# Attention stage of a four-block kernel: GpSimd adds the coarse weights to the fine ones in place, and one set of wide products sums them

## The reference

```python
for lvl, (ql, kl, vl) in enumerate(qkvs):
    if lvl == 0:
        A = jnp.exp(S)                                  # S masked, less its row maximum
        y = jnp.einsum('bnij,bnjd->bnid', A, vl)
        Av = A.sum(-1)
    else:
        A = jnp.exp(S)                                  # q of odd blocks, k of even blocks
        y = jnp.einsum('bnij,bnjd->bnid', A, v1b)
        Av = A.sum(-1)
        y, Av = each padded with zeros to even blocks, and repeated 2 ** lvl times
    seq_key = (idx >> lvl << lvl) + (2 ** lvl - 1)
    keep = seq_key <= idx                               # the last token of each group of 2 ** lvl
    Ysum = Ysum + jnp.where(keep[None, :, None], y, 0.0)
    Asum = Asum + jnp.where(keep[None, :], Av, 0.0)
out = Ysum / (Asum + EPS)[..., None]
```

## Time and profile before

| What | us |
|---|---|
| median of 3 executions | 697.13 |
| lowest and highest | 693.63 and 697.72 |
| the profiled execution, its own time | 694.56 |
| its span in the trace | 692.7 |

### The profile page before, as it was taken

One profiled execution on the slowest core, in us unless ns is written; L12 is line 12 of the kernel. 1 busy time (PEld: TensorE's weight loads), 2 busy tenths in 40 slices (PEclk: granted clock), 3 DMA queues, 4 the chain that ended last, 5 costly groups with the idle time before them and its releaser, 6 DMA issues.

```text
span 692.7 us, 17766 instructions
## 1 busy us (share of the span) xinstructions
PE 531.0 (77%) x6946; PEld 317.5 (46%) x6948; DVE 435.2 (63%) x881; ACT 286.8 (41%) x621; POOL 247.8 (36%) x247
## 2 busy tenths in 40 slices
PE   0768686474758997289999999999997656569991
PEld 0213232143434433157777677777766544344330
DVE  1477969883513564647788888878788466125552
ACT  3442432234114664465444455444444152127660
POOL 1367767652270666310111111211111223704662
PEclk9998797855698999599999999999999556979997
DMA  5999200000061883300001000001000000525854
GB/s 146 395 382 106 30 1 0 0 1 0 11 188 35 216 238 106 100 12 14 18 18 34 17 18 18 18 18 30 21 7 8 1 0 1 157 76 147 229 174 136
DMA packets 43601, 54.16 MB, mean 78 GB/s; under 512 B 10816, under 2 KB 34176, under 8 KB 42496
## 3 DMA queue, kind: packets, MB, share of 16 engines
q1 hardware_dynamic: 40960, 47.78, 24.9%
q0 software_dynamic: 2560, 5.26, 2.1%
HBM read 43.55 MB, written 9.48 MB: 77 GB/s over the span
## 4 chain that ended last, share of the span: by engine, by line
PE 65%; DVE 12%; issue 7%; ACT 5%; POOL 5%; DMA 2%; another core or an unknown queue 2%; SPq 1%; DVEq 0%; POOLq 0%; ACTq 0%
PE psum L1291 9%; PE psum L900 7%; PE psum L1309 6%; PE psum L1372 5%; PE psum L1346 4%; PE psum L1330 4%; PE psum L916 4%; PE psum L857 3%; PE psum L865 3%; DVE arena L621 3%; PE psum L907 2%; POOL arena L529 2%; PE psum L1362 2%; PE psum L257 2%; PE psum L1354 2%
## 5 line engine op out<-in xcount | busy, mean ns | idle before, releaser
L1640 POOL TENSOR_TENSOR arena<-arena 128x1024 f32<-128x1024 f32 x16 | 37.8, 2362 | 211.0 <-DVE arena L1562 211.0
L1135 POOL DMA_INDIRECT y_tok<-arena,to x48 | 55.2, 1149 | 70.8 <-ACT arena L976 65.8
L1291 PE MATMUL psum<-arena 128*128 128x512 f32 x128 | 62.8, 633 | 1.3 <-ACT arena L1429 1.0
L529 POOL TENSOR_TENSOR arena<-arena 128x512 f32<-128x512 f32 x32 | 51.4, 1628 | 30.3 <-DVE arena L621 30.3
L1446 ACT ACTIVATE arena<-psum 128x512 f32<-128x512 f32 x64 | 38.1, 597 | 37.2 <-PE psum L1291 37.2
L621 DVE TENSOR_TENSOR_SCAN arena<-arena 128x512 f32<-128x512 f32 x32 | 53.0, 1698 | 0.0
L900 PE MATMUL psum<-experts,arena 128*32 x96 | 50.0, 602 | 2.9 <-issue 1.9
L900 PE MATMUL psum<-arena 128*32 128x512 f32 x288 | 50.9, 605 | 0.0
L1309 PE MATMUL psum<-arena 128*128 128x128 f32 x384 | 46.6, 278 | 1.0 <-ACT arena L1451 1.0
L1570 DVE TENSOR_TENSOR x_tok<-x_tok,psum 128x512 f32<-128x512 f32 x32 | 22.0, 688 | 39.5 <-PE psum L1372 39.5
L981 ACT ACTIVATE arena<-experts 128x768 f32 x48 | 40.4, 845 | 14.3 <-issue 14.2
(11 more groups left out here) (197 smaller groups left out, 1185.2 us busy)
## 6 DMA issues: line engine op xcount, KB each, us to landing
arena<-in_experts SPq DMA_DIRECT2D x48, 384.0 KB
experts<-in_experts SPq DMA_DIRECT2D x8, 1536.0 KB, 19.5
arena<-sorted_x SPq DMA_DIRECT2D x48, 64.5 KB
sorted_x<-zeros SPq DMA_DIRECT2D x2, 1536.0 KB, 22.5
arena<-in_w_qkv SPq DMA_DIRECT2D x16, 192.0 KB, 3.2
arena<-y_tok SPq DMA_DIRECT2D x8, 256.0 KB, 3.7
arena<-in_w_out SPq DMA_DIRECT2D x16, 64.0 KB, 1.9
out<-x_tok SPq DMA_DIRECT2D x4, 256.0 KB, 2.7
```

The lines of the kernel that those rows point to most:

```text
L529: pool.tensor_tensor(a_g[m % HALF], a_r[c % 2], a_state[:, m, 0:CHUNK], ALU.mult).then_inc(s["g"], 1)
L1135: pool.indirect_dma_start(out=y_tok, out_offset=bass.IndirectOffsetOnAxis(ap=f_to[:, s:s + 1], axis=0), in_=f_gy[s % 4], in_offset=None).t ...
L1291: pe.matmul(ring("in", n, j)[:, :], b_w[n % 2][:, which * P:which * P + P], x, start=True, stop=True)\
```

## The change

The 22 narrow Z products of each unit are gone. GpSimd adds the coarse weights onto the fine ones inside b_e (merge), in five additions for each unit: 256, 128, 64, 32 and 32 elements in each partition, the last in half of the partitions. Each addition reads 16 neighbouring coarse weights at a time and 16 fine ones that stand 2, 4, 8, 16 or 32 columns apart, and writes these in place. From the second on, each waits for the one before. The four wide Z products then sum fine and coarse weights together (add_weights), and stand behind the Y products of weighted(n, ROUGH).

The additions of unit n wait for its coarse exponentials (expd) and for its fine Y products, which read b_e before it is changed (weighed, a new semaphore that counts twice in each unit behind the Y products). summed now counts once in each unit. copy_y and the drains of the values wait for weighed in place of summed. On GpSimd, merge(n+1) stands behind the product of unit n.

```diff
+        MERGES = LEVELS
...
+        def merged_columns(a):
+            fine = a[:, 0:2 * CHUNK].rearrange("p (h t) -> p h t", h=2)
+            rough = a[:, 2 * CHUNK:QK].rearrange("p (h i k) -> p h i k", h=2, k=D_B)
+            one = rough[:, :, 0:2].rearrange("p h i (g s) -> p h (i g) s", s=16)
+            two = rough[:, :, 2].rearrange("p h (g s) -> p h g s", s=16)
+            three = rough[:, :, 3, 0:32].rearrange("p h (g s) -> p h g s", s=16)
+            return [(fine.rearrange("p h (g c s) -> p h g c s", c=32, s=2)[:, :, :, 16:32, 1], one),
+                    (fine.rearrange("p h (g c s) -> p h g c s", c=32, s=4)[:, :, :, 16:32, 3], two),
+                    (fine.rearrange("p h (g c s) -> p h g c s", c=32, s=8)[:, :, :, 16:32, 7], three),
+                    (fine[:, :, 256 + 15:512:16], rough[:, :, 3, 32:48]),
+                    (fine[64:128, :, 31:512:32], rough[64:128, :, 3, 48:64])]
...
-                if not rough:
-                    after(pe, h["z_out"], n)
-                    for head in range(2):
-                        for r in range(2):
-                            rows, out = slice(64 * r, 64 * r + 64), slice(64 * head, 64 * head + 64)
-                            mm = pe.matmul(Z[r][out], b_ones[rows], b_e[n % 2][rows, head * CHUNK:head * CHUNK + CHUNK],
-                                           start=True, stop=False)
-                else:
-                    for i in range(part.start, part.stop):
-                        for head in range(2):
-                            for r in range(2):
-                                rows, out = slice(64 * r, 64 * r + 64), slice(64 * head, 64 * head + 64)
-                                for cols, place in places(r, i):
-                                    mm = pe.matmul(place(Z[r][out]), b_ones[rows], e[rows, head, i - part.start, cols],
-                                                   start=False, stop=last_place(r, i, cols))
...
+                mm.then_inc(h["weighed"], 1)
+
+            def add_weights(n):
+                pe.wait_ge(h["merged"], MERGES * n + MERGES)
+                after(pe, h["z_out"], n)
+                for head in range(2):
+                    for r in range(2):
+                        rows, out = slice(64 * r, 64 * r + 64), slice(64 * head, 64 * head + 64)
+                        mm = pe.matmul(Z[r][out], b_ones[rows], b_e[n % 2][rows, head * CHUNK:head * CHUNK + CHUNK],
+                                       start=True, stop=True)
                 mm.then_inc(h["summed"], 1)
...
                     weighted(n, ROUGH)
+                    add_weights(n)
...
-                    after(act, h["summed"], 2 * (n - 1) - 1 if j < 7 else 2 * (n - 1))
+                    after(act, h["weighed"], 2 * (n - 1) - 1 if j < 7 else 2 * (n - 1))
...
-                act.wait_ge(h["summed"], 2 * n + 2)
+                act.wait_ge(h["weighed"], 2 * n + 2)
...
-                after(dve, h["summed"], 2 * (n - 2) + rough + 1)
+                after(dve, h["weighed" if rough else "summed"], 2 * (n - 2) + 2 if rough else n - 1)
...
-                dve.wait_ge(h["summed"], 2 * n + 2)
+                dve.wait_ge(h["summed"], n + 1)
...
+            def merge(n):
+                pool.wait_ge(h["expd"], 2 * n + 2)
+                pool.wait_ge(h["weighed"], 2 * n + 1)
+                for j, (whole, some) in enumerate(merged_columns(b_e[n % 2])):
+                    if j:
+                        pool.wait_ge(h["merged"], MERGES * n + j)
+                    pool.tensor_tensor(whole, whole, some, ALU.add).then_inc(h["merged"], 1)
...
+                if n == 0:
+                    merge(0)
...
                 pool.tensor_tensor(b_yn, b_y, b_rec, ALU.mult).then_inc(h["normed"], 1)
+                if n + 1 < UNITS:
+                    merge(n + 1)
```

More of the change, by code:

```diff
@@ L1197, in hybrid_block @@
         h = {n: sem("b_" + n) for n in (
-            "shift xn xt x pooled packed packed_odd ready coarse proj drained scored subbed turned expd summed y_out z_out divided normed o "
+            "shift xn xt x pooled packed packed_odd ready coarse proj drained scored subbed turned expd weighed merged summed y_out z_out divided normed o "
             "acc").split()}
@@ L1345, in weighted @@
                             for cols, place in places(r, i):
-                                pe.matmul(place(Y[r][out]), b_v[n % 2][rows, i, out], e[rows, head, i - part.start, cols],
-                                          start=(i == 0), stop=last_place(r, i, cols))
-                if not rough:
-                    after(pe, h["z_out"], n)
-                    for head in range(2):
-                        for r in range(2):
-                            rows, out = slice(64 * r, 64 * r + 64), slice(64 * head, 64 * head + 64)
-                            mm = pe.matmul(Z[r][out], b_ones[rows], b_e[n % 2][rows, head * CHUNK:head * CHUNK + CHUNK],
-                                           start=True, stop=False)
-                else:
-                    for i in range(part.start, part.stop):
-                        for head in range(2):
-                            for r in range(2):
-                                rows, out = slice(64 * r, 64 * r + 64), slice(64 * head, 64 * head + 64)
-                                for cols, place in places(r, i):
-                                    mm = pe.matmul(place(Z[r][out]), b_ones[rows], e[rows, head, i - part.start, cols],
-                                                   start=False, stop=last_place(r, i, cols))
+                                mm = pe.matmul(place(Y[r][out]), b_v[n % 2][rows, i, out], e[rows, head, i - part.start, cols],
+                                               start=(i == 0), stop=last_place(r, i, cols))
+                mm.then_inc(h["weighed"], 1)
[7 more added lines that the diff above has]
+                                       start=True, stop=True)
                 mm.then_inc(h["summed"], 1)
```

## The result

| What | before | changed |
|---|---|---|
| median of 20 executions each, us | 697.38 | 697.9 |
| ratio, with its 95% interval | | 1.0067 (1.0035 to 1.0100) |
| span of the profiled execution, us | 692.7 | 696.3 |
| a unit in the steady state, us | 15.01 | 15.01 |
| unit 0, from its first fine Y product to the next maximum, us | 5.3 | 6.5 |

The forecast was 0.9 us faster; measured is no gain, and by the ratio a slightly slower kernel. The ratio leaves out executions in a slower state; over all twenty of each kernel the medians give 697.9 / 697.38 = 1.0007 and the means 697.16 / 695.68 = 1.0021, so 1.0067 is not to be read as the size of the effect. The lengths inside the stage are the firmer measure.

What follows compares the result with a forecast made beforehand. TensorE was taken to bound the attention stage, busy 199.23 of 200 us. Steady units -2.0, unit 0 +1.0 and the last unit +0.1 sum to -0.9 us: 696.2 us, range 690.5 to 706.

Steps and rivals of the forecast that it cites:

- M: Time of the five GpSimd additions in a unit with their hand-overs: 2.36 us forecast, break-even at 2.50.
- Step (1): Narrow Z products gone from TensorE: 1.01 us a unit, 14.1 us in all, as the ceiling.
- Step (2): Wide Z products no longer cover GpSimd's product: projection starts 0.4 us earlier, not 0.97; gain capped at 0.43 us a unit.
- step (7): Earlier event for copy_y and the value drains, VectorE's moved work, TensorE's clock in short waits: counted at nothing.
- Step (3): Additions on GpSimd: 0.25 us fixed each, 1.55 ns an element, 2.36 us with hand-overs.
- Rival B: Spread elements are read more slowly on GpSimd: M = 2.56, +2.1 us, 699.2 us; chance 0.20.
- Step (4): TensorE's wide products wait for the additions: 0.14 us gained a unit, 2.0 us in all; lateness passes one for one.
- The signs: Two TensorE waits a unit: 0.5 us before the projection, 0.3 before the wide products; second missing means C.
- C: Additions hidden, fixed part small: M = 1.93, TensorE waits for GpSimd's product only, -5.4 us, 691.7 us; chance 0.15.
- Step (5): Unit 0, with no output projection to hide the additions: 1.0 us lost, once.
- Step (6): Last unit: additions hidden before the divide that ends the stage; 0.1 us lost, at most 1.
- Rival A: Additions as slow as products beside VectorE scans: M = 3.35, unit 0.85 us longer, 711.1 us; chance 0.20.

Runs made afterwards that it cites:

- e3: Changed kernel with the wide Z products moved behind the next unit's fine scores: unit 14.34 us, ratio 0.9883 to before.
- e9: e3 with ScalarE's last copy of values ahead of the coarse exponentials and VectorE's coarsen ahead of gather_out: unit 14.31 us, ratio 0.9903 to before.
- e2: Changed kernel without the five additions and TensorE's wait for them: unit 14.91 us, ratio 1.0001 to before.
- e6: e2 with ScalarE's last copy of values moved ahead of the coarse exponentials: unit 14.78 us.
- e4: Changed kernel with one more GpSimd addition of 256 neighbouring elements in each unit, ahead of the five: unit 15.73 us.
- e1: Changed kernel again, no edit: unit 15.00 us, unit 0 7.7 us, ratio 1.0088 to before.
- c1: Kernel of before, unchanged, timed against itself: unit 15.01 us, ratio 1.0073.

## Why the prediction was wrong

The order of what ends last was right. The sizes were not: the forecast lived on 0.14 us a unit, and 0.14 was lost. Two chains had to be shorter for a gain, and neither gave what it was to give. Over the additions (steps 3 and 4) nothing was left, as M was 2.48 and the wide products 1.02. Over TensorE (steps 1 and 2) the most was 0.10 us and not 0.43, so even with M at 2.36 the gain could not have been more than 14 x 0.10 = 1.4 us. From the maximum, the projection starts 0.42 us earlier than before (9.34 for 9.76), takes 0.13 longer (2.12 for 1.99), and from coarse Y to the mask it takes 0.29 longer (2.00 for 1.71, of which 0.09 are the additions): the sum is nothing.

- Step (1), the ceiling: 1.01 us for the narrow products. Measured 0.70, as coarse Y alone is 1.01 (e3, e9) and not 0.70. Start-to-start differences gave the tail of one group to the next one. e9, where TensorE is the bound, has a unit of 15.01 - 0.70 = 14.31 us.
- Step (2), the wait for GpSimd's product: right to 0.04 us. The cap of 0.43 us that followed from it was wrong, and measured 0.10 (e2). Of the 0.33 lost, 0.24 is the uneven tail: 1.91 against 1.67 us from coarse Y to the mask. 0.13 is a wait that step (7) had at nothing: the second half of the projection needs the bank of ScalarE's last copy of values (e6). The projection's earlier start gave 0.04 back.
- Step (3), the additions: 2.36 forecast, 2.48 measured. The fixed part was too long (0.25, where a line through the forms of 32 and 64 gives 0.19) and the price of an element too low: 1.55 ns forecast; taking 0.19 off, (0.742 - 0.19) / 256 = 2.2 ns at two columns apart and (0.525 - 0.19) / 128 = 2.6 at four. Neighbours cost (0.61 - 0.19) / 256 = 1.6 (e4). Rival B was the right mechanism: its M was 2.56. The fixed part was shorter than it had, and so M stayed under it. "GPSIMD Engine Reference" of the Trainium skill, "Performance pitfalls for Q7 kernels", has reads more than 8 bytes apart at about half as much again; here such elements cost 2.6 ns against 1.6, which roughly agrees. It counts a step of 8 bytes as free, and here it costs 2.2 against 1.6; the measurement decides. The additions write apart as well as read apart, and no run tells the one from the other.
- Step (4): pass-through one for one, right (e4). The mask came at 13.46 us after the maximum, not at 454.15 - 440.83 = 13.32. Of the 0.14, 0.12 is the additions, 0.05 the wide products at 1.02 in place of 0.97, and -0.03 a shorter hand-over (0.05 for 0.08). The signs did not all serve: a second wait of 0.3 us, before the wide products, was to tell this case from C. The timeline shows none, yet C did not hold, because coarse Y took 0.3 us longer than I had it and filled the time. The first wait was 0.37 us for the 0.5 forecast.
- Step (5), unit 0: 1.0 forecast. 1.2 to 1.4 measured where the clock stays, and 2.4 to 2.6 where it falls (e1). The additions begin 325.74 - 324.37 = 1.37 us behind the first fine Y product and not 316.54 - 315.48 = 1.06: the start of the next group had been taken for the end of fine Y. That TensorE's waits do not endanger its clock was right for the units between (1.00 from 338 to 540 us) and wrong for this one. The first fine Y product in before and in the changed kernel:

```profile
315.48 1.16 PE L1346 MATMUL psum<-arena 64*64 64x64 f32 x64
```

```profile
324.37 2.01 PE L1359 MATMUL psum<-arena 64*64 64x64 f32 x108
```

- Step (6): right within what the traces can tell; the time from GpSimd's 15th product to the end of the stage was 17.5 to 17.8 us before and 17.2 to 18.1 after.
- Rival A would have made a unit 0.85 us longer and C 0.43 shorter; neither occurred, with M at 2.48.

By the stage, before took 268.9, 268.9 and 268.2 us and the changed kernel 270.5 and 269.7, on average 1.4 more. Unit 0 gives about +2.0, the steady state -1.0, and the way to unit 0 +0.4. The -1.0 is one unit of before that was 16.08, 16.36 and 15.54 us long in its three profiles, always the step into GpSimd's 13th product. TensorE pauses there for nothing that the profile shows, as this row of c1 has it (who waited, for whom, us in total, times, longest):

```profile
PE psum L1330 <- issue: 1.1, 1, 1.1
```

The changed kernel has 15.3 and then 14.8 near there. What makes that pause was not tried, so it stays open whether its absence belongs to the change.

1.4 us are a ratio of 1.002, which is also the ratio of the means over all twenty executions. The measured 1.0067 and 1.0088 are more. Parts outside the stage differ by as much between two profiles of one kernel; whether a small steady part of it belongs to the change stays open.

## What to carry to other kernels

Work taken off the bounding engine is worth what that engine saves when the group behind the removed one is run without it; start-to-start differences in a trace give a group the tail of the one ahead, so look for a place in the same trace where the group stands alone, or list the last starts of one group beside the first starts of the next. Removing a cover makes every later event on that path earlier, so list each wait inside the uncovered group, not only the one at its head. If a new producer ends just in time, first move its consumer behind work that does not need it: the same change in another place made 1% where in the first place it made nothing.

## What the runs showed that I had not expected

- Identical kernels differ by some 6 us from one execution to the next, by when TensorE's products come to their full pace in the first 40 us (line 237: 638 or 1134 ns). A 95% interval from a dozen runs did not cover it (1.0031 to 1.0115 for no change).
- VectorE pays for GpSimd's additions where they meet: pair sums of 0.28 us took 0.36 in the steady state, 0.75 in unit 0 and 0.83 in e9. "SBUF — State Buffer" of the Trainium skill, "Who interferes with whom", has the later of two such instructions wait for the whole of the earlier one. The trace agrees as to who waits: the 0.36 ends at 448.44, 0.14 us behind the last addition (448.30), and the 0.83 ends at 441.04, 0.15 us behind the first (0.74 us from 440.15). It goes the other way too: in e4 the last addition of GpSimd, which starts with a pair sum at 456.29, takes 0.41 us and not 0.27.
- On VectorE the five additions take 1.65 us and on GpSimd 2.48.
